# A two-layer decoder with mixture-of-experts layers: layer-one routing and gathering as side steps of the context-attention loop

## The reference

```python
logits = einsum('btc,ce->bte', x, router_w) + router_b        # x is the normalised row; 8 experts
top_k_logits, expert_indices = top_k(logits, 2)
probs = softmax(top_k_logits)
# per sequence: first choices of all tokens come before second choices
one_hot = one_hot(swapaxes(expert_indices, 0, 1).ravel(), 8)
pos = cumsum(one_hot, axis=0) * one_hot - 1                     # the token's slot in its expert
buf = zeros((8, cap, 256)).at[expert, pos].add(x)              # cap = 33; what does not fit is dropped
h, g = buf @ w_c_fc + b_c_fc, buf @ w_gate + b_gate             # per expert, 256 to 1024
o = silu(h * g) @ w_c_proj + b_c_proj                           # 1024 to 256
out = sum_k probs[k] * o[expert_k, min(pos_k, cap - 1)]
```

## Time and profile before

| | us |
|---|---|
| median of 3 runs (lowest, highest) | 1946.52 (1944.9, 1956.92) |
| the profiled execution, its own time | 1952.73 |
| span of that execution in the trace | 1951.1 |
| PE busy | 1719.9 |
| DVE busy | 1177.2 |
| ACT busy | 828.2 |
| POOL busy | 452.9 |

### The profile page before, as it was taken

How to read it: one execution, slowest core, us unless ns; L and a number is a source line. 1 busy time by engine, 2 the same in 40 slices (tenths; PEclk the granted TensorE clock), 3 DMA queues, 4 the chain that set the end, 5 groups by cost and what they waited for, 6 DMA issues and landing times. The chain is left out here.

```text
span 1951.1 us, 39011 instructions
## 1 busy us (share of the span) xinstructions
PE 1719.9 (88%) x13070; PEld 1375.2 (70%) x13070; DVE 1177.2 (60%) x2667; ACT 828.2 (42%) x2420; POOL 452.9 (23%) x710
## 2 busy tenths in 40 slices
PE   3887689999998687799999949999999759999998
PEld 2555456666666476688888837777787649999996
DVE  3887546777777443366666534666665365666657
ACT  1332345555555123244444424444444245554534
POOL 1111201222222222212112021111111006544523
PEclk9999789999999699799999969999999879999999
DMA  8000133333350433000000000000000122312101
GB/s 241 0 0 0 55 93 125 119 123 123 123 171 11 151 119 120 20 11 13 11 9 12 4 24 24 17 16 16 21 10 1 40 90 70 126 66 93 37 1 38
DMA packets 87656, 114.20 MB, mean 59 GB/s; under 512 B 4832, under 2 KB 77071, under 8 KB 87311
## 3 DMA queue, kind: packets, MB, share of 16 engines
q1 hardware_dynamic: 82382, 99.91, 16.0%
q0 software_dynamic: 5184, 13.11, 2.0%
HBM read 65.04 MB, written 47.97 MB: 58 GB/s over the span
## 5 line engine op out<-in xcount | busy, mean ns | idle before, releaser
L1215 PE MATMUL ps<-e_ex_high,e_w_high 128*128 128x264 f32 x512 | 146.8, 287 | 5.4 <-POOL e_w_low L2475 5.4
L1215 PE MATMUL ps<-e_ex_high,e_w_low 128*128 128x264 f32 x512 | 146.5, 286 | 0.0
L1215 PE MATMUL ps<-e_ex_low,e_w_high 128*128 128x264 f32 x512 | 146.2, 286 | 0.0
L931 ACT ACTIVATE c_probs<-ps,c_negmax 112x375 f32<-112x375 f32 x256 | 143.7, 581 | 2.1 <-DVE c_negmax L1028 2.1
L1028 DVE TENSOR_REDUCE c_negmax<-ps 112x2 f32<-112x750 f32 x128 | 114.2, 934 | 34.7 <-PE ps L1152 34.7
L1814 PE MATMUL ps<-xnT,s_qkv 128*128 (+1 forms) x1024 | 130.5, 285 | 2.0 <-DVE xnT L1661 1.0
L1121 PEld LDWEIGHTS ps<-const,c_probs 112*125 112x125 f32 x768 | 99.0, 193 | 45.3 <-DVE c_pT L1044 19.4
L1814 PEld LDWEIGHTS ps<-xnT,s_qkv 128*128 128x128 f32 x1024 | 123.2, 199 | 6.4 <-DVE xnT L1661 1.7
L1628 ACT ACTIVATE s_probs<-ps,s_negmax 112x112 f32<-112x112 f32 x256 | 86.7, 365 | 74.8 <-DVE s_negmax L1677 74.8
L1121 PE MATMUL ps<-const,c_probs 112*125 112x112 f32 x768 | 115.1, 287 | 3.5 <-DVE c_pT L1044 2.0
L2004 ACT ACTIVATE c_probs<-ps,c_negmax 112x375 f32<-112x375 f32 x128 | 71.7, 574 | 83.1 <-DVE c_negmax L2060 83.1
(11 more groups left out here) (361 smaller groups left out, 4600.2 us busy)
## 6 DMA issues: line engine op xcount, KB each, us to landing
expert_rows<-d_zero SPq DMA_DIRECT2D x16, 2240.0 KB, 12.1
c_ctx_in<-in_ctx SPq DMA_DIRECT2D x32, 375.0 KB
e_wgt<-in_L_ffn_w_gate SPq DMA_DIRECT2D x8, 1024.0 KB, 5.0
e_wfc<-in_L_ffn_w_c_fc SPq DMA_DIRECT2D x8, 1024.0 KB, 7.2
e_wpj<-in_L_ffn_w_c_proj SPq DMA_DIRECT2D x8, 1024.0 KB, 9.6
e_x_in<-expert_rows SPq DMA_DIRECT2D x44, 128.0 KB, 2.0
expert_rows<-e_y POOLq DMA_DIRECT2D x44, 128.0 KB, 2.0
s_qkv<-in_L_attn_W_qkv SPq DMA_DIRECT2D x1, 3072.0 KB, 11.2
```

The source lines that it names most:

```text
L931: last = nc.scalar.activation(probs[:, g % 2, r, :], ps[:T, r, 0:S], ACT.Exp, bias=negmax[:, par, h:h + 1], accum_out=sums[:, par, h:h + 1])
L1215: last = nc.tensor.matmul(out, a, b, start=start and n == 0, stop=stop and n == len(pairs) - 1)
```

## The change

The routing and the gathering of layer one's experts leave `experts_1` and become side steps in `context_attention_1` (class `Dispatch1`). Iteration i now also has `logits` and `ranks` of sequence i-2 (both through the bank that DVE empties) and `slots0` and `slots1` of sequence i-3 (the one that ACT empties). DVE finds the two best experts with `max` and `max_index`, marks them in `hot`, and from the ranks makes the slots and two small rows `sel`; POOL makes the one-hot matrix from `hot` and `sel` in three operations; PE makes the two slot products, and ACT copies them into `ex`. `XN` and its write are gone, the iterations run to i = 18, and those from -3 to 4 and from 13 on are written out. Expert 0's weights are loaded at the start of `context_attention_1`, expert 1's at the start of the experts' block. In that block DVE and ACT make the probabilities (`diff`, an exponential, `held`, three small operations). `experts_0` has `BLOCKS` = 43. Keys, queries and values of `self_attention_1` lie in memory of `e0.gate_up`, and the order of the first loads is another.

```diff
-BLOCKS = 2 * ROWS // TILE + E0
+BLOCKS = (2 * ROWS - E0) // TILE + E0
...
-    side = Side([("result", -1, ON_DVE), ("query", 1, ON_ACT), ("key0", 1, ON_DVE), ("context0", 2, ON_ACT),
-                 ("key1", 1, ON_DVE), ("key2", 1, ON_ACT),
-                 ("key3", 1, ON_DVE), ("value0", 1, ON_ACT), ("value1", 1, ON_DVE), ("context1", 2, ON_ACT),
+    side = Side([("result", -1, ON_DVE), ("query", 1, ON_ACT), ("slots0", -3, ON_ACT), ("key0", 1, ON_DVE), ("context0", 2, ON_ACT),
+                 ("slots1", -3, ON_ACT), ("key1", 1, ON_DVE), ("logits", -2, ON_DVE), ("key2", 1, ON_ACT),
+                 ("key3", 1, ON_DVE), ("value0", 1, ON_ACT), ("value1", 1, ON_DVE), ("ranks", -2, ON_DVE), ("context1", 2, ON_ACT),
...
             def iteration(i, par):        # POOL
...
                 split_context(1, i, par)
+                if within(i - 2):
+                    dispatch.keep_best(pool, i - 2, par)
+                    dispatch.one_hot(pool, i - 2)
...
             def iteration(i, par):        # ACT
...
                 evacuate("query", i, par)
+                evacuate("slots0", i, par)
                 copy_probs(i, 0, 1)
                 evacuate("context0", i, par)
+                evacuate("slots1", i, par)
                 copy_probs(i, 0, 3)
...
             def iteration(i, par):        # DVE
...
                 evacuate("key1", i, par)
-                rows_ready(i)
+                evacuate("logits", i, par)
+                rows_ready(i, 1 - par)
                 maxima(i, 1)
+                if within(i - 2):
+                    dispatch.mark_experts(dve, i - 2, (side_done[ON_DVE], side.done("logits", i)))
                 evacuate("key3", i, par)
...
                 copy_probs(i, 1, 2)
+                evacuate("ranks", i, par)
+                if within(i - 2):
+                    dispatch.select_slots(dve, i - 2, (side_done[ON_DVE], side.done("ranks", i)))
                 evacuate("rows", i, par)
                 evacuate("inverse", i, par)
...
             def iteration(i, par):        # PE
...
                 aside("key0", i, par)
+                aside("slots0", i, par)
+                transposes(i, 0, 2)
                 aside("context0", i, par)
-                transposes(i, 0, 2)
                 aside("key1", i, par)
                 transposes(i, 0, 3)
+                aside("slots1", i, par)
+                aside("logits", i, par)
                 aside("key2", i, par)
...
                 transposes(i, 1, 2)
+                aside("ranks", i, par)
                 aside("context1", i, par)
                 aside("rows", i, par)
```

More of the change, by code:

```diff
@@ L44, in constant_columns @@
     put("count16", np.tile(np.arange(16, 0, -1), (T, 1)))
-    put("slots", np.tile(np.arange(CAP), (T, 1)))
+    put("slots", np.tile(np.arange(1, CAP + 1), (T, 1)))
     put("upto", np.triu(np.ones((T, T))))
@@ L1516, in within, with sequences_ahead, self_attention_1 @@
     return not isinstance(q, int) or 0 <= q < B
-def sequences_ahead(eng, ahead, iteration):
-    for i in range(-ahead, 1):
+def sequences_ahead(eng, ahead, iteration, behind=0):
+    start = 2 * behind + 1
+    for i in range(-ahead, start):
         iteration(i, i % 2)
-    with eng.Fori(1, B - 4, 2) as i:
+    with eng.Fori(start, B - 4, 2) as i:
         iteration(i, 1)
         iteration(i + 1, 0)
-    for i in range(B - 3, B + 1):
+    for i in range(B - 3, B + 1 + behind):
         iteration(i, i % 2)
-def self_attention_1(nc, sh, w):
+def self_attention_1(nc, sh, w, spare):
     H, DH, HALF = 16, 64, 4 * T
@@ L1892, in context_attention_1 @@
+def context_attention_1(nc, sh, w, e1):
     H, DH, SC = 8, 64, NK * T
@@ L1982, in evacuate @@
                 act.wait_ge(side_mm[ON_ACT], side.done(name, i))
-                if name == "query":
+                if name in ("slots0", "slots1"):
+                    last = dispatch.take_slots(bank_act, i - 3, int(name[-1]))
+                elif name == "query":
                     last = nc.scalar.copy(qT[:, 1 - par, :, :], bank_act[:, 0:4 * T].rearrange("p (m t) -> p m t", m=4))
@@ L2171, in aside @@
                     for c in range(2):
-                        last = nc.tensor.transpose(bank[:, c * T:(c + 1) * T], xn[:, c * 128:(c + 1) * 128], ident[:T, :T])
+                        last = nc.tensor.transpose(bank[:, c * T:(c + 1) * T], dispatch.xn[:, 1 - par, c * 128:(c + 1) * 128], ident[:T, :T])
+                elif name in ("slots0", "slots1"):
+                    last = dispatch.slot_products(pe, bank, i - 3, 1 - par, int(name[-1]))
+                elif name == "logits":
+                    last = dispatch.logits(pe, bank, i - 2, par)
+                elif name == "ranks":
+                    last = dispatch.rank_products(pe, bank, i - 2)
                 elif name == "query":
@@ L2354, in experts_1 @@
+        ex = sh.ex
+        held = sb("held", [T, B, 2])
+        prob = sb("prob", [T, 2, B])
+        diff = sb("diff", [T, B])
+        diff_ready, ediff_ready, chain = sem("diff_ready"), sem("ediff_ready"), sem("chain")
+        w1 = ExpertWeights(lambda name, shape: sb(name + "_odd", shape))
+        weights, w_in = (w.even, w1), w.w_in
         sel = sb("sel", [T, 2, CAP])
@@ L2620, in matrix @@
                     link = chained(dve, comb_chain, b * 2)
-                    one_hot(dve, link, held, b, True)
+                    one_hot(dve, link, b)
                     if later:
```

286 lines of the change are left out of this document (139 added, 147 removed).

## The result

The changed kernel took 1980.97 us in the median of 4 runs (1977.73 to 1992.03), the kernel before 1949.38 (4 runs) on the same chip: a ratio of 1.0164, interval 1.0118 to 1.0211. Timed again in a later series of six runs it was 1.0133, interval 1.0098 to 1.0169. So the change costs 26 to 32 us, where I had forecast 11 and a range that ended at 1976.

What follows compares the result with a forecast made beforehand. The prediction took the loop to be bound by PE (22.57 us of work in 22.81). Its terms, -55.5 + 16.9 + 5.8 + 45.7 - 1.6 = +11.3 us, took the median from 1946.52 to 1957.8, range 1936 to 1976.

Steps and rivals of the forecast that it cites:

- What goes: Between context attention's end and the first expert product: all 55.5 us of routing, gathering and block start go, -55.5.
- block start: From the last slot copy to the first expert product: 4.67 us before, taken as 5.8 after the change.
- The tail: Behind the loop, iterations 16 to 18 run serially for the last sequences' routing: from 8.8 to 25.7 us, +16.9.
- at full clock the four slot passes are half of 1.13: PE's slot products in each loop iteration: four passes priced at 0.5 us.
- The small products: PE's logits and ranks in each iteration, three fp32 products each: 0.65 and 0.6 us.
- Hole A: At x = 2 in the loop, PE idles for ACT's copies of slots0 and of probabilities x = 1: +1.0 us.
- Hole B: At the iteration's end, PE idles before ranks (0.6) and inverse (0.5); value1 to value2 grows by 1.2 us.
- Sum of the loop: Context attention loop: +3.4 us per full iteration, 41 for twelve, +2 in iteration 2, +2.9 in iteration 15: +45.7.
- One tile fewer: In experts_0, one step fewer at 1.74 us each: -1.6 us.
- Rival 2: GpSimd's one-hot and VectorE's context normalisations hold each other up in the loop: +25 us, 1972; chance 0.22.
- Rivals 1 and 3: Rival 1: only passes cost, no holes, 1934, chance 0.22; rival 3: loop takes steps almost for nothing, 1920, chance 0.08.
- The likeliest case: Whole kernel: the forecast itself, 1957.8 us, reaching from 1948 to 1968, chance 0.48.

Runs made afterwards that it cites:

- e3: Changed kernel with 8 instead of 264 columns in each slot product, the other columns left out; 1972.24 us, 1.0079 of the kernel before.
- e1: Changed kernel with ACT's copy of the probabilities x = 1 put ahead of its copy of slots0; 1975.94 us, 1.0100 of the kernel before.
- e11: Changed kernel with all context attention iterations written out, no hardware loop; 1981.85 us, 1.0161 of the kernel before.
- e4: Changed kernel with the three one-hot operations on VectorE, behind inverse, instead of GpSimd; 1983.56 us, 1.0149 of the kernel before.
- e7: e6 with the one-hot matrix made by one VectorE comparison instead of two selections and three GpSimd operations; 1965.83 us, 1.0063 of the kernel before.
- e6: Changed kernel with the reorderings of e1 and e2, and iteration 17's logits of sequence 15 ahead of sequence 14's slots; 1966.40 us, 1.0070 of the kernel before.
- e8: Kernel before the change with 43 tiles in experts_0 and its one-hot matrix made by one comparison instead of five operations; 1942.48 us, 0.9942 of the kernel before.
- e10: e8 run again unaltered; 1939.58 us, 0.9934 of the kernel before.
- e2: Changed kernel with PE's ranks behind context1 and DVE's row copy ahead of the slot selection; 1977.06 us, 1.0097 of the kernel before.
- e5: Changed kernel once more, unaltered; 1980.68 us, 1.0133 of the kernel before.

## Why the prediction was wrong

The sign and the mechanism were right, and the size was off by 15 to 20 us.

- **What goes, block start.** -55.5 stands. From the end of the last slot copy (1634.37 + 0.38) to the first expert product (1640.70) it is 5.95, where I had 5.8. No expert waited for weights.
- **The tail: +16.9, measured +19.7** (28.50 against 8.78). The forecast's own terms end at +25.5 and not +25.7, which changes nothing here. Up to the copy of the last rows it was right (12.0 after the last `c_invT`, forecast 12.1), and GpSimd's one-hot (0.64 twice and 0.74 per sequence) was near my 0.8. What was short is the price of the slot products. These are the last two.

```profile
1631.39 1.22 PE L1978 MATMUL ps<-d_oneh,d_xn 112*128 112x264 f32 x2 [4.04 <-POOL d_oneh L1973]
1632.64 0.38 ACT L1982 COPY ex<-ps 128x264 f32<-128x264 f32 x1 [8.82 <-PE ps L1978]
...
1633.08 1.25 PE L1978 MATMUL ps<-d_oneh,d_xn 112*128 112x264 f32 x2 [0.47 <-ACT ex L1982]
```

One product (two passes) takes 1.22 at the low clock, not the 0.6 of the forecast. Two pairs stand in the tail one behind the other: +2.5, nearly all that was missing. In the second profile the tail was 30.3, 1.8 longer, all of it ahead of the copy of the last rows (13.8 after the last `c_invT`). Most of that is the last output product, which took 3.48 at a granted clock of 0.53 instead of 1.95 at 1.00.

- **The failed step: "at full clock the four slot passes are half of 1.13".** The row of four passes in 1.13 was taken for the lower clock level, since the clock of the stretch around it was mixed. But within that stretch the clock had risen, and the row lies in its later half, as this view of the kernel before shows.

```profile
1576.41:1590.00 13.59, 10.72 (x32) 6.90 (x32) 11.92 (x40) 7.04 (x23) 0.00 (x0) 0.84 0.00 1
1590.00:1604.35 14.35, 9.12 (x32) 5.42 (x32) 10.91 (x36) 7.80 (x25) 0.00 (x0) 1.00 0.00 0
```

  So 1.13 was the price at full clock already. e3 measured it: 0.57 for taking away 256 of 264 columns in four passes. From start to start the four passes take 1.0, where I had 0.5. One wrong reading cost about 0.5 in each of 13 iterations (6.5 us) and 2.5 in the tail, half of the whole miss.
- **The small products** (logits and ranks, 12 passes): I had 0.65 and 0.6. From the start of the first pass to the start of the next product, logits take 0.73 and ranks 0.61. Nearly right, 1 us in all.
- **Hole A: +1.0.** Measured 0.99 on PE's matmuls, 0.7 of it recoverable (e1). Right.
- **Hole B: +1.2 from `value1` to `value2`.** It was 1.7 (5.51 from start to start instead of 3.81), and 1.4 in the iterations written out (5.23). The place and the releasers are as forecast. Too short in the forecast were the gaps between dependent DVE operations: 0.15 and 0.26 in an iteration written out, 0.26 and 0.27 in the hardware loop. Of the 0.5 too little, 0.2 stand in every full iteration (2.5 us), and 0.3 are part of the next point.
- **The hardware loop: not in the sum.** In iterations 3, 4 and 13, written out, the period was 27.0 in the second profile, so 4.2 over before against a forecast of 3.4; in the eight of the hardware loop 27.5. This is +0.5 each, 4 us, and e11 shows it. I had read the loop as a way of writing, because the kernel before has the same period of 22.8 in both forms. That it costs nothing under a busy PE says nothing of a chain of handoffs.
- **Sum of the loop.** 6.5 + 1 + 2.5 + 4 = 14, and 45.7 + 14 = 60 against 401.5 - 341.3 = 60.2 in the second profile. The first has 63.4, with two full iterations at clocks of 0.94 and 0.98 (1.9 us) and the last period 1.2 longer.
- **One tile fewer: -1.6.** The products of that stage ran 86 passes instead of 88. The first stretch is 2.0 shorter in the first profile; nothing contradicts it.
- **Rival 2** (GpSimd and VectorE). The three context normalisations did take 1.43 and 1.88 in turn beside the one-hot instead of 1.05, but `c_oT` came behind `values` anyway; e4 and e7 show that the loop pays nothing. The Trainium skill's SBUF — State Buffer (the section on the two separate sides) says that the shared port pair is held for a whole instruction and the loser fully blocked. For the normalisations the trace agrees: in the two iterations looked at, each of the four that began while a GpSimd operation ran ended 0.15 after it. What blocked the rounding in the experts' block lasted over ten GpSimd instructions, 7.43 us. By the rule as worded it would have waited for one, 0.75.
- **Rivals 1 and 3** fell with both holes.

The likeliest case reached to 1968, and the range to 1976, because its upper end came from a rival, not from the prices that were least sure. (Its lower end, 1936, was said to be rival 1, whose own sum gives 1934.) All errors of price went the same way: passes, handoffs and a loop form were each taken at the value that they have when PE is full and at full clock.

## What to carry to other kernels

Before an operation's row is used as a price, read the granted clock of just that stretch, since a mean of 0.9 over a longer one hides both levels; a factor of two in one row was half of this miss. Moving serial work into a loop whose bounding engine is full pays for every pass at full price and adds waits of a few tenths that did not exist while the others were early. Here 27.9 to 29.7 us were saved behind the loop and 60 to 63 lost in it, and no order of the steps that was tried got below 1.007 of the kernel before (e6), or 1.006 with the one comparison (e7). What made the block outside the loop shorter was to compute less: one comparison instead of five operations brought 7 us there at once. With one tile fewer, this version beats both kernels (e8 0.9942, e10 0.9934, and 0.9916 with GpSimd paced, which these runs don't tell from the other two).

## What the hardware did that I had not expected

**A rounding on VectorE that waits for all of GpSimd's row.** In 5 of the 12 profiles without pacing the first rounding of `e_hid_high` took 7.43 to 7.92 us, in the other seven the longest took 1.03 to 1.10, and nothing lay between. The experts' block was 306.7 to 307.6 with it, and 298.1 to 298.9 without. It was the first of the 64 roundings each time, and ended 0.3 after the end of an unbroken row of 24 GpSimd operations (0.75 us each, 0.69 apart). In the other seven the first rounding got in between and overlapped at most three of them. The kernel before shows it too, in the form of e8. That the two engines' phase decides it was only argued, and the traces don't bear it out in its simple form: the long ones began 0.45 to 0.63 after the start of a GpSimd operation, the others 0.21 to 0.63, and at 0.60 and at 0.63 both outcomes occurred. What decides it stays open.

**The clock took back what reordering won.** In the kernel before, all twelve full iterations had a granted clock of 1.00, in the second profile of the changed kernel too. In e1, e2, e3, e6, e7 and e11, all with shorter periods than the changed kernel's, it fell below 0.99 in three to seven of the full iterations (a fall that lies on a mark counts in two). In the first profile of the changed kernel it fell in two. These windows of e6 show one such iteration, first the end of the one before it, then its start.

```profile
1401.62:1403.62 2.00, 1.75 (x14) 1.42 (x12) 1.53 (x4) 0.83 (x2) 0.87 (x1) 1.00 0.00 0
1403.62:1405.62 2.00, 1.44 (x11) 1.22 (x11) 1.00 (x6) 0.82 (x2) 0.98 (x2) 1.00 0.00 0
1405.62:1433.71 28.09, 26.91 (x183) 21.53 (x182) 16.01 (x43) 11.49 (x30) 6.04 (x9) 0.93 0.04 14
1405.62:1407.62 2.00, 2.00 (x6) 1.28 (x4) 1.76 (x5) 0.00 (x0) 1.31 (x3) 0.52 0.00 0
1407.62:1409.62 2.00, 2.00 (x25) 1.72 (x24) 0.81 (x2) 0.58 (x1) 0.66 (x1) 0.63 0.04 3
```

PE was busy for 1.44 of the last 2 us before the fall, at hole B, with no single wait over 0.41, then ran near the lower level of 1.2 GHz for less than 4 us, and the iteration took 28.09 instead of 26.28. The changed kernel has more idle time at the same place and kept its clock in e5, so idle time alone doesn't explain it. Why some kernels' loops lose the clock and others don't stays open.
